# GpSimd's add of the two rotation products, 512 columns at once or 2 x 256

## The reference, cut to what matters

```python
k_rope = heads(x @ W_krope, ROPE_DIM)
q_rope = heads(q_c @ W_qrope, ROPE_DIM)
def _apply_rope(x, cos, sin):
    d2 = x.shape[-1] // 2
    x1, x2 = (x[..., :d2], x[..., d2:])
    rot = jnp.concatenate([-x2, x1], axis=-1)
    return x * cos[None, None, :, :] + rot * sin[None, None, :, :]
```

## Time and profile before

| | |
|---|---|
| median of 3 runs | 3761.25 us (3760.82 to 3765.47) |
| the profiled execution, its own time | 3765.83 us |
| its span, first to last instruction | 3763.9 us |
| TensorE, matmuls | 3497.9 us busy, 93% of the span |
| VectorE | 2277.2 us, 61% |
| ScalarE | 1914.9 us, 51% |
| GpSimd | 958.1 us, 25%, 1069 instructions |
| mean granted TensorE clock | 0.950 of full speed |

### The profile page before, as it was taken

The page is one execution under the profiler, slowest core; times in us unless marked ns, Lnnn a source line. Parts: engine busy times, 40 slices in busy tenths (PEclk is TensorE's granted clock), DMA queues, the critical chain, the costliest instruction groups (busy, mean ns, idle before and its releaser), DMA issues.

```text
span 3763.9 us, 63193 instructions
## 1 busy us (share of the span) xinstructions
PE 3497.9 (93%) x24928; PEld 2034.2 (54%) x24928; DVE 2277.2 (61%) x4778; ACT 1914.9 (51%) x2947; POOL 958.1 (25%) x1069
## 2 busy tenths in 40 slices
PE   4788999999999999999999999999999999999876
PEld 3354555565555556555555655555565555555443
DVE  3446575666756566675656667565666756566442
ACT  2234645546464554646455464645546464564422
POOL 2212132322313232231323223132321313232111
PEclk8788999999999999999999999999999999999977
DMA  3000000000000000000000000000000000000000
GB/s 91 1 1 1 1 1 12 1 12 1 12 1 1 12 1 12 1 9 4 1 12 1 12 1 7 7 1 12 1 12 1 5 9 1 12 1 7 1 6 6
DMA packets 40881, 27.72 MB, mean 7 GB/s; under 512 B 19600, under 2 KB 39696, under 8 KB 40592
## 3 DMA queue, kind: packets, MB, share of 16 engines
q1 hardware_dynamic: 40592, 23.69, 2.2%
HBM read 15.30 MB, written 8.39 MB: 6 GB/s over the span
## 4 chain that ended last, share of the span: by engine, by line
PE 78%; DVE 13%; ACT 4%; issue 2%; POOL 2%; DVEq 0%; POOLq 0%; ACTq 0%
PE ps L478 72%; PE ps L489 6%; DVE G L954 3%; DVE XN L843 3%; DVE MX L915 2%; ACT PR L1174 2%; DVE MX L909 2%; DVE stats L834 1%; POOL PR L1304 1%; POOL rstd L1246 1%; DVE X L861 1%; ACT ATT L1192 0%; DVE G L952 0%; ACT other L1093 0%; DVE MAT L921 0%
## 5 line engine op out<-in xcount | busy, mean ns | idle before, releaser
L1174 ACT ACTIVATE PR<-ps 128x1024 f32<-128x1024 f32 (+3 forms) x592 | 522.4, 931 | 308.4 <-PE ps L478 306.0
L478 PE MATMUL ps<-MAT 32*128 32x512 f32 (+5 forms) x4928 | 580.2, 491 | 13.0 <-DVE MAT L921 3.8
L915 DVE TENSOR_REDUCE MX<-ps 128x2 f32<-128x1024 f32 (+3 forms) x512 | 392.4, 820 | 300.9 <-PE ps L478 300.4
L1246 POOL TENSOR_TENSOR rstd<-var,neg_half 128x4 f32<-128x4 f32 x144 | 150.1, 1043 | 1375.5 <-DVE var L826 1236.1
L478 PEld LDWEIGHTS ps<-MAT 32*128 32x128 f32 (+2 forms) x4928 | 289.1, 196 | 246.5 <-issue 159.6
L478 PE MATMUL ps<-XT,cn_w 128*128 128x256 f32 x1536 | 365.8, 392 | 13.7 <-DVE XT L853 10.4
L478 PEld LDWEIGHTS ps<-XT,cn_w 128*128 128x128 f32 x1536 | 291.5, 194 | 92.0 <-issue 37.2
L478 PE MATMUL ps<-other,cn_w 128*128 128x512 f32 (+2 forms) x1152 | 318.0, 481 | 21.6 <-ACT other L1104 6.5
L921 DVE SCALAR_TENSOR_TENSOR MAT<-ps,MAT 128x512 f32<-128x512 f32 x128 | 88.2, 689 | 346.8 <-PE ps L489 346.2
L909 DVE TENSOR_REDUCE MX<-ps 128x2 f32<-128x1024 f32 (+6 forms) x256 | 220.4, 904 | 126.5 <-PE ps L478 125.9
L1304 POOL TENSOR_SCALAR_AFFINE_SELECT PR<-PR 128x512 f32<-128x512 f32 (+1 forms) x192 | 166.2, 865 | 430.5 <-ACT PR L1174 430.5
(11 more groups left out here) (158 smaller groups left out, 5753.1 us busy)
## 6 DMA issues: line engine op xcount, KB each, us to landing
X<-in_L_attn_x SPq DMA_DIRECT2D x16, 512.0 KB, 3.9
out<-X SPq DMA_DIRECT2D x16, 512.0 KB, 2.9
w_up<-in_L_attn_W SPq DMA_DIRECT2D x1, 1024.0 KB, 7.2
w_down<-in_L_attn_W SPq DMA_DIRECT2D x1, 1024.0 KB, 8.8
w_krope<-in_L_attn_W_krope SPq DMA_DIRECT2D x1, 512.0 KB, 4.7
w_qk<-in_L_attn_Wqkv SPq DMA_DIRECT2D x4, 128.0 KB, 4.2
cn_w<-in_L_ffn_cn_w SPq DMA_DIRECT2D x1, 256.0 KB, 4.2
w_qrope<-in_L_attn_W_qrope SPq DMA_DIRECT2D x1, 256.0 KB, 2.8
```

The lines of the kernel that those rows point to most:

```text
L478: return pe.matmul(dst, lhsT, rhs, start=start, stop=stop, skip_group_check=True)
L915: last = dve.tensor_reduce(MX[:, t, at], src[:, :, a:a + nk[pair]], AX_X, ALU.max)
L1174: freed(act.activation(PR[0:m, tile_of((s, q, g, r)), 2 * pair:2 * pair + 2, lo:T], ps[0:m, b:b + 2, 0:T - lo], ACT.Exp, scale=SCALE[s]), ...
L1246: pool.tensor_tensor(rstd[:, c, :], var[:, c, :], neg_half[:], ALU.pow).then_inc(rstd_ready.sem, 1)
```

## The change

One instruction of `rotated` becomes two. The first half of the tokens is added, then the second, with no wait between them, and the signal for both hangs on the second. The words that come with the change also say that GpSimd's wait for the last exponentials is for the second pair of heads; the diff has no line on that.

```diff
@@ -1278,7 +1278,10 @@
                     read_out(pool, "rope", q, g, w)
                     pool.wait_ge(rope_turned.sem, rope_turned.at(q, g, w))
                     dst = MAT[:, rope_tile(("B", q, g), w), :]
-                    pool.tensor_tensor(dst, a, b, ALU.add).then_inc(rope_sum.sem, 1)
+                    for v in range(2):
+                        tok = slice(v * T // 2, (v + 1) * T // 2)
+                        last = pool.tensor_tensor(dst[:, tok], a[:, tok], b[:, tok], ALU.add)
+                    last.then_inc(rope_sum.sem, 1)
                     before = hi_before["B", q, g]
```

## The result

| | before | after |
|---|---|---|
| median | 3761.25 us | 3738.10 us (3736.36 to 3740.84, 3 runs) |
| ratio, 95% interval | | 0.9934 [0.9915, 0.9954] |
| profiled execution, its span | 3765.83, 3763.9 us | 3740.84, 3738.8 us |
| TensorE, matmuls busy | 3497.9 us | 3482.4 us |
| mean granted clock | 0.950 | 0.955 |

A forecast was written before the change was run, and what follows sets the result against it. TensorE was taken to bound the kernel (78% of the span on the path), GpSimd counting only where its tiles or stalls reach TensorE. Terms of -14 and +2.7 gave -11.3 us: 3750 us, range 3745 to 3768.

The forecast's parts named there:

- The cost of halves: GpSimd's rotation adds: a half takes 0.73 us, so each split add costs 0.13 us more.
- Group 0: TensorE's first weight load of max.B.0.0 comes 0.12 us later, 16 times; with the first sequence's loads +2.7 us.
- Rival B: Group 0's k, q chain: the second instruction costs much more; at 0.4 us extra +13 us, 3774; chance 0.12.
- Groups 1 and 2: No effect: VectorE waits for a projection anyway in one, TensorE's load follows its own work in the other.
- Group 3's hand-over: VectorE passes between the q add's halves; the seventh weighted sum ends 1.0 us earlier, 14 times: -14 us.
- Who wins the meeting: Group 3: VectorE's fourth weighted sum, 0.05 us ahead of GpSimd's wide operation instead of 0.19 behind, goes first.
- rival A: Group 3: the fourth weighted sum is still caught by the wide operation; only +2.7 us stays, 3764; chance 0.33.
- The sum: Whole kernel: -14 + 2.7 = -11.3 us, 3750 us against the median; chance 0.45.
- Rival C: The wait for the second pair of exponentials isn't in the diff and would cost nothing; chance within forecast and rival A.

The follow-up runs named there:

- e2: Kernel before with the seven other adds of a sequence in halves and the q add of group 3 whole: 3764.12 us, ratio 1.0003.
- e1: Kernel before with only the q add of group 3 in halves: 3739.49 us, ratio 0.9943.
- e3: Changed kernel plus a 0.21 us GpSimd memset between the halves of group 3's q add: 3762.71 us, ratio 1.0001 to the kernel before.
- e9: Kernel before, whole adds, plus a useless GpSimd memset of 384 columns just ahead of group 2's wide operation: 3737.25 us, ratio 0.9933.
- e5: Kernel before with three matmuls of zeros in TensorE's idleness ahead of mout.F: 3740.14 us, ratio 0.9941.
- e10: The changed kernel timed once more against the kernel before: 3742.18 us, ratio 0.9941.
- e7: Kernel before, whole adds, with the two bias steps of F moved to just ahead of group 3's k turn: 3692.76 us, ratio 0.9818.
- e4: Kernel before with six matmuls of zeros while TensorE waits for the last weighted sum: 3759.94 us, ratio 0.9993.

## Why the prediction fell short, step by step

- **The cost of halves** was right: 0.73 us each, 1.41 for two in group 0 where one took 1.27, so 0.14 more where 0.13 was said. Rival B is out.
- **Group 0** was right: outside group 3's stretch a sequence takes 0.12 us more in the profile of the change and 0.14 in e2, and nothing more in e1, where group 0 is whole. It costs 2 us.
- **Groups 1 and 2** bring nothing: with their adds in halves e2 is 0.14 us a sequence slower, about what group 0 costs.
- **Group 3's hand-over** was right in its chain and its size: fourth sum at 7.30 (7.31 forecast), seventh ends at 12.01 (12.02). It is 1.0 us in 13 of 14 sequences, -13 us. e1 and e2 show that it is this add alone, e3 and e9 that it is worth this only through the meeting with the wide operation.
- **Who wins the meeting** was called by the earlier trace rows with a threshold of VectorE 0.01 later. That was wrong for this pair of operations: the one at 0.047 us earlier was caught (profile of the result), the one at 0.049 went through (e1). The forecast lead of 0.05 was on that edge, and the real one, 0.055 to 0.074 in the 13 sequences, was just enough; rival A was 0.01 to 0.03 us away. That the forecast won over rival A was luck. What decides within these hundredths was not found. The Trainium skill (SBUF — State Buffer, "SBUF: two separate sides") says that whichever starts first gets the pair; by the recorded starts that holds only to within these hundredths.
- **The sum: the term of group 3 stopped at mout.F, and this is what failed.** "1.0 us off TensorE's 3.31 of idleness, 14 times: -14 us" puts the granted clock at nothing, without a reason. In before TensorE works under a granted clock of half speed for some 10 us, in two stretches, around and behind this idleness in most sequences. The stretch from the seventh sum to L921 takes 16.63 us in before and 16.05 in after, mean of 14 each (15.94 in e1): 14 x 0.58 = 8 us. e5 shows that the idleness sets off the first of the two: work put into the gap takes mout.F to 1.99 us in 13 of 14 sequences, with the sums where they were. How much of the 8 us the shorter idleness brings each time is less sure: 2.3 us of it still leave mout.F at 2.44 to 2.82 in all of e1, and in e2 and e3, where the sums end as in before, the stretch was 16.49 and 16.48. The rest of a period (q add to q add, less that stretch) went from 203.53 to 202.72: -0.93 for the sums, +0.12 for group 0.

Together -13 - 8 + 2 = -19 us by the profiles. In the profiled execution another 5.3 us are already won by 382 us, before B and F meet. That is not shown to be the change's: e5, which leaves those sequences alone, has 5.1 of it in its profile, e9 4.3 and e3 2.6, while e2 and e10, which split the adds there, have none (0.2 and 1.1 later than before). The gain goes with the clock: ahead of 390 us the low stretches add up to 137 us in before, 133 in e2 and e10, 126 in e3 and 116 in after, e5 and e9. The interval of the result, 17 to 32 us, holds the 19; the other 4 of the 23 us have no cause shown.

Rival C stands as it was: the wait for the exponentials was not in the diff, so what it would do was not measured.

## What to carry to other kernels

Where two engines stall each other, write down the starts and ends of both in a row and look for the meeting whose order decides. Moving operations that nobody waits for out of that row (e7, 69 us) was worth more here than cutting one in the middle of it (23 us). Price an idleness of TensorE with the slow clock behind it: here 2.75 us of useless matmuls in the gap gave 21 us over 14 gaps. A gain that hangs on 0.02 us is not safe; count in the trace how often it comes out.

## What the runs showed that I had not expected

- A 0.42 us memset on GpSimd made the kernel 28 us faster (e9), and a 0.21 us one undid the whole gain (e3).
- A 512-column float32 matmul of 64 rows took 0.89 us in e4 (5.32 us for six) and 0.92 in e5 (2.75 for three), and is recorded as two instructions; I had counted 0.43.
- The second low stretch of the clock, some 10 us after the first (low from 1464.1 and from 1474.3 us in before), stayed in e4 and e5 although the idleness ahead was filled. What sets it off was not tried.
